# Gated MLP: normalised rows split in row layout and turned by DMA transposes, with three pairs of up banks and two up tiles ahead of the second product

## The reference

```python
x = x + o @ wo
h = shift_token(x)            # second half of the features is taken from the row before
mu = h.mean(-1, keepdims=True)
var = h.var(-1, keepdims=True)
h = (h - mu) / jnp.sqrt(var + 1e-05) * lg + lb
h = h @ w1 + b1               # 256 -> 2 * 682
a, g = jnp.split(h, 2, axis=-1)
h = a * jax.nn.gelu(g, approximate=False)
x = x + h @ w2 + b2           # 682 -> 256
```

## Time and profile before

| what | value |
|---|---|
| median of three executions | 4295.84 us |
| span of the profiled execution | 4300.7 us |
| PE busy in the span | 3849.4 us (90%) |
| DVE, ACT, POOL busy | 3344.8, 2570.4, 1178.2 us |
| first MLP stage | about 1304 to 1508 us of the span |
| second MLP stage | about 1958 to 2161 us of the span |

### The profile page before, as it was taken

The page is one execution under the profiler, slowest core; times in us unless marked ns, Lnnn a source line. Parts: engine busy times, 40 slices in busy tenths (PEclk is TensorE's granted clock), DMA queues, the critical chain, the costliest instruction groups (busy, mean ns, idle before and its releaser), DMA issues. The chain is left out here.

```text
span 4300.7 us, 95101 instructions
## 1 busy us (share of the span) xinstructions
PE 3849.4 (90%) x38420; PEld 2181.8 (51%) x38420; DVE 3344.8 (78%) x5499; ACT 2570.4 (60%) x3473; POOL 1178.2 (27%) x958
## 2 busy tenths in 40 slices
PE   7999999669998969988986899999999999857996
PEld 4788888535555535555553332332333333434764
DVE  5688888769985569985787989999998978585454
ACT  3566666636654335553443777787888888635563
POOL 1122321267761067771140000000000000013552
PEclk9999999889999989999997999999999999978998
DMA  1010100133330033430062000000000000032444
GB/s 63 5 40 28 43 26 25 41 70 65 63 51 28 0 64 65 66 54 8 0 160 47 9 9 1 9 2 2 9 2 2 9 2 9 4 99 76 89 106 104
DMA packets 291062, 167.00 MB, mean 39 GB/s; under 512 B 204692, under 2 KB 281704, under 8 KB 290152
## 3 DMA queue, kind: packets, MB, share of 16 engines
q1 hardware_dynamic: 268040, 125.49, 13.4%
q0 software_dynamic: 13440, 21.24, 2.8%
q10 hardware_dynamic: 9184, 14.68, 1.0%
HBM read 77.81 MB, written 38.58 MB: 27 GB/s over the span
## 5 line engine op out<-in xcount | busy, mean ns | idle before, releaser
L2257 DVE TENSOR_REDUCE s_tops<-ps 128x2 f32<-128x1024 f32 (+3 forms) x1152 | 1251.0, 1131 | 139.9 <-PE ps L2143 101.0
L2226 ACT ACTIVATE s_weights<-ps 128x1024 f32<-128x1024 f32 (+3 forms) x1152 | 1092.6, 952 | 342.2 <-PE ps L2156 191.7
L2178 PE MATMUL ps<-s_weights,v_flat 128*32 128x256 f32 (+1 forms) x8704 | 690.8, 389 | 7.4 <-ACT s_o_t L2232 6.1
L2137 PE MATMUL ps<-keys,s_q 48*128 48x512 f16 (+3 forms) x2304 | 433.3, 373 | 46.9 <-DVE s_tops L2257 27.2
L2156 PE MATMUL ps<-s_q,keys 50*128 50x512 f16 (+3 forms) x2304 | 433.4, 373 | 46.0 <-DVE s_tops L2257 33.6
L2293 POOL CAST s_shift<-s_minus_top 128x16 f16<-128x16 f32 x32 | 6.3, 196 | 1426.8 <-DVE s_minus_top L2264 1426.8
L583 PE MATMUL ps<-a_qt,a_kt 128*128 128x256 f16 x3072 | 375.3, 273 | 3.8 <-POOL s_ones L538 3.8
L2156 PEld LDWEIGHTS ps<-s_q,keys 50*128 50x128 f16 x2304 | 112.2, 93 | 510.1 <-issue 250.1
L1174 PE MATMUL ps<-attention_w,la_yt 128*128 128x512 f16 x1152 | 290.3, 400 | 37.8 <-DMA la_yt<-la_y_parts 30.4
L583 PEld LDWEIGHTS ps<-a_qt,a_kt 128*128 128x128 f16 x3072 | 300.9, 98 | 40.3 <-POOL s_ones L538 4.2
L1249 ACT ACTIVATE la_weights<-ps 128x1024 f32<-128x1024 f32 x124 | 126.8, 1023 | 297.0 <-PE ps L1164 297.0
(11 more groups left out here) (374 smaller groups left out, 7205.5 us busy)
## 6 DMA issues: line engine op xcount, KB each, us to landing
ex_whole<-in_L_ffn_w_dram ACTq DMA_DIRECT2D x14, 1024.0 KB
qk_parts<-a_parts SPq DMA_DIRECT2D x64, 128.0 KB, 4.2
keys<-qk_parts SPq DMA_DIRECT2D x48, 128.0 KB, 5.5
s_q<-qk_parts SPq DMA_DIRECT2D x48, 128.0 KB, 4.7
x<-in_x_dram SPq DMA_DIRECT2D x8, 512.0 KB, 9.4
attention_w<-attention_split SPq DMA_DIRECT2D x2, 2048.0 KB, 9.1
la_table<-in_rotary_dram SPq DMA_DIRECT2D x64, 64.0 KB, 2.1
a_table<-in_rope_dram POOLq DMA_DIRECT2D x8, 512.0 KB, 6.3
```

Of the source, the lines that this page charges most:

```text
L2137: mm = pe.matmul(m.ps[:, bank, 0:width], b.q[rows(half, KEY_PARTS * L1_DH), place % 2, pair, t * P:(t + 1) * P], m.keys[rows(half, KEY_PAR ...
L2178: mm = pe.matmul(m.ps[h * QUAD:(h + 1) * QUAD, OUT, begin:end], m.v_flat[:, first:first + QUAD], weights[:, a % 2, h, begin:end], start=(k ...
L2226: act.activation(weights[:, a % 2, 2 * pair:2 * pair + 2, skip:CHUNK], m.ps[:, bank:end + 1, skip:CHUNK], ACT.Exp).then_inc(s["exp"], 1)
L2257: dve.tensor_reduce(tops[:, u % 2, :, i % 2, t, c], m.ps[:, bank:end + 1, 0:width], AX.X, ALU.max).then_inc(s["max"], 1)
```

## The change

The turn goes from PE to the DMA engines, and three other things move with it.

- `gain` on POOL multiplies `normed` by a row of `ln_g` and adds a row of `ln_b`, in place (two operations of 128x1024 a chunk). For the first chunk DVE does it. Both rows are loaded by SP at the start, replicated on all partitions.
- `high` on ACT casts the chunk to the high f16 part in row layout (`parts`), one operation of 128x1024, behind the gelu of tile 2. `parts_low` on DVE subtracts to get the low part, one operation of 128x1024, behind the gate work of tile 3.
- `turn` on SP waits for `low` and issues 4 DMA transposes, one for each row tile, each of 128 rows by 512 f16 values (128 KB). `up` waits for all four. The shift by one row for the second feature half is now made by reading `ht` one column earlier (`EDGE - k`), and `edge` on POOL copies the column of the row before.
- Banks 0 and 1 are free, so there are three pairs of up banks (`RING = 3`), and PE makes two up tiles of the next chunk ahead of `down` (`AHEAD = 2`).

```diff
-    TURN_AT = ET - 4
+    RING, AHEAD = 3, 2
+    EDGE = 16
+    HIGH_AT, LOW_AT = 2, 3
...
             def _(sp):
+                for to, name in ((lng_row, "ln_g"), (lnb_row, "ln_b")):
+                    sp.dma_start(to[:, :], layer_of(a[name], layer).rearrange("o d -> (o d)").partition_broadcast(P)).then_inc(s["rows_in"], 16)
...
+                def turn(c):
+                    sp.wait_ge(s["low"], c + 1)
+                    if c:
+                        need(sp, s["ht"], 16 * TPC * c)
+                        need(sp, s["a_mm"], ET * (c - 1))
+                    for j in range(TPC):
+                        at = EDGE + j * P
+                        sp.dma_start_transpose(ht[:, c % 2, :, :, at:at + P].rearrange("p a k t -> p (a k) t"),
+                                               parts[:, c % 2, j, :, :].rearrange("p a d -> p (a d)")).then_inc(s["ht"], 16)
+
+                turn(0)
                 move_down(sp, m, s, 1)
                 if not last:
                     load_attention(sp, m, a, layer + 1, s["next_in"])
                 move_up(sp, m, s, 1)
+                for c in range(1, CHUNKS):
+                    turn(c)
...
+                def gain(c, u):
+                    need(pool, s["normed"], c + 1)
+                    whole = normed[:, u, :, :]
+                    pool.tensor_tensor(whole, whole, lng_row[:, :].unsqueeze(1).broadcast_to([P, TPC, D]), ALU.mult).then_inc(s["gained"], 1)
+                    pool.wait_ge(s["gained"], c)
+                    pool.tensor_tensor(whole, whole, lnb_row[:, :].unsqueeze(1).broadcast_to([P, TPC, D]), ALU.add).then_inc(s["whole"], 1)
...
-                def ht_low(c, u):
-                    need(dve, s["a_mm"], ET * (c - 1))
-                    for k in range(KD):
-                        need(dve, s["ht_high"], KD * c + k + 1)
-                        dve.tensor_tensor(ht[:, u, 1, k, :], ht_whole[:, u, k, 0:CHUNK], ht[:, u, 0, k, :], ALU.subtract).then_inc(s["ht"], 1)
+                def parts_low(c, u):
+                    dve.wait_ge(s["high"], c + 1)
+                    dve.tensor_tensor(parts[:, u, :, 1, :], normed[:, u, :, :], parts[:, u, :, 0, :], ALU.subtract).then_inc(s["low"], 1)
...
-                        if e == TURN_AT + 1 and exists(c + 1):
-                            ht_low(c + 1, 1 - u)
+                        if e == LOW_AT and exists(c + 1):
+                            parts_low(c + 1, 1 - u)
...
+                def high(c, u):
+                    if isinstance(c, int) and c == 0:
+                        act.wait_ge(s["first_whole"], 1)
+                    else:
+                        act.wait_ge(s["whole"], c)
+                        need(act, s["ht"], 16 * TPC * (c - 1))
+                    act.copy(parts[:, u, :, 0, :], normed[:, u, :, :]).then_inc(s["high"], 1)
...
-                        if e == TURN_AT and exists(c + 1):
-                            scaled(c + 1, 1 - u)
+                        if e == HIGH_AT and exists(c + 1):
+                            high(c + 1, 1 - u)
...
                 def up(c, u, tiles):
-                    need(pe, s["ht"], KD * (c + 1))
+                    need(pe, s["ht"], 16 * TPC * (c + 1))
...
-                            need(pe, free, ET * c + e - 2 + 1)
+                            need(pe, free, ET * c + e - RING + 1)
...
                 def step(c, u):
-                    up(c, u, range(1, TURN_AT + 1))
+                    up(c, u, range(AHEAD, ET))
                     if exists(c + 1):
-                        turn(c + 1, 1 - u)
-                    up(c, u, range(TURN_AT + 1, ET))
-                    if exists(c + 1):
-                        up(c + 1, 1 - u, range(1))
+                        up(c + 1, 1 - u, range(AHEAD))
                     down(c, u)
```

More of the change, by code:

```diff
@@ L1442, in gated_mlp @@
         after = statistics_buffers(nc, ctx, "gm") if last else None
-        with stage(nc, f"gm{layer}", "weighted", "x", "consts", *(f"x_{n}" for n in STATISTICS), "next_in", "w2_in", "minus", "first", *ROW_STATISTICS, "zeroed", "before", "normed", "turned", "ht_whole", "ht_high", "ht", "a_mm", "g_mm", "gelu",
+        with stage(nc, f"gm{layer}", "weighted", "x", "consts", *(f"x_{n}" for n in STATISTICS), "next_in", "w2_in", "minus", "first", *ROW_STATISTICS, "zeroed", "before", "edge_high", "edge_low", "edge", "normed", "rows_in", "first_gained", "first_whole", "gained", "whole", "high", "low", "ht", "a_mm", "g_mm", "gelu",
                    "hid_whole", "hid_high", "hid", "out", "b2", "y") as (block, s):
@@ L1491, in _ @@
             def _(dve):
-                credit(dve, s["normed"], s["ht"], s["hid_whole"], s["hid"], s["y"])
+                credit(dve, s["normed"], s["hid_whole"], s["hid"], s["y"])
                 def norm(c, u, rows=range(TPC)):
-                    need(dve, s["turned"], KD * (c - 1))
+                    if not isinstance(c, int) or c >= 2:
+                        dve.wait_ge(s["low"], c - 1)
                     for j in rows:
@@ L1615, in _, with hid_high @@
             def _(act):
-                credit(act, s["ht_whole"], s["ht_high"], s["gelu"], s["hid_high"])
+                credit(act, s["gelu"], s["hid_high"])
                 act.wait_ge(s["first"], 1)
-                act.activation(ht_whole[:, 1, 1, CHUNK:CHUNK + 1], m.ps[:, 7, 0:1], ACT.Identity, bias=b.lnb[:, 1:2],
-                               scale=b.lng[:, 1:2]).then_inc(s["before"], 1)
+                act.activation(before[:, :], m.ps[:, 7, 0:1], ACT.Identity, bias=b.lnb[:, 1:2], scale=b.lng[:, 1:2]).then_inc(s["before"], 1)
                 act.wait_ge(s["before"], 1)
[L1623 to L1634, removed]
+                act.copy(ht[:, 0, 0, 1, EDGE - 1:EDGE], before[:, :]).then_inc(s["edge_high"], 1)
+                def high(c, u):
[5 more added lines that the diff above has]
+                    act.copy(parts[:, u, :, 0, :], normed[:, u, :, :]).then_inc(s["high"], 1)
                 def gelus(c, u):
-                    def high(e):
+                    def hid_high(e):
                         need(act, s["hid_whole"], ET * c + e + 1)
@@ L1659, in _ @@
             def _(pe):
[L1660 to L1664, removed]
-                        need(pe, s["ht_whole"], KD * (c - 1) + k + 1)
-                        for j in range(TPC):
-                            t = pe.transpose(m.ps[:, k, j * P:(j + 1) * P], normed[:, u, j, k * P:(k + 1) * P], m.ident[:, :])
-                        t.then_inc(s["turned"], 1)
+                credit(pe, s["a_mm"], s["g_mm"], s["out"])
                 def up_rest(c, u, e):
-                    need(pe, s["gelu"], ET * c + e - 2 + 1)
-                    need(pe, s["hid_whole"], ET * c + e - 2 + 1)
+                    need(pe, s["gelu"], ET * c + e - RING + 1)
+                    need(pe, s["hid_whole"], ET * c + e - RING + 1)
                     terms = [(k, p, q) for k in range(KD) for p, q in TERMS]
@@ L1683, in up @@
                 def up(c, u, tiles):
-                    need(pe, s["ht"], KD * (c + 1))
+                    need(pe, s["ht"], 16 * TPC * (c + 1))
+                    if isinstance(c, int) and c == 0:
+                        pe.wait_ge(s["edge_low"], 1)
+                    else:
+                        need(pe, s["edge"], c)
                     for e in tiles:
```

55 lines of the change are left out of this document (39 added, 16 removed).

## The result

| what | before | after |
|---|---|---|
| median of four executions | 4296.35 us | 4401.71 us (4393.78 to 4403.22) |
| ratio, 95% interval (the quotient of the two medians is 1.0245) | | 1.0234 [1.0221, 1.0246] |
| span of the profiled execution | 4300.7 us | 4401.3 us |
| MLP stage 1, from the `pick` matmul to the end of the last down | 202.9 us | 251.5 us |
| MLP stage 2, the same | 202.3 us | 248.5 us |

Of the 100.6 us between the two spans 94.8 lie in the two MLP stages. Another 4.6 lie behind the second stage, and 1.1 ahead of the first and between the two.

The account below looks back on a forecast made before the run. PE, working nearly without a gap, was taken as the bound. 2 x (17.5 + 31.4 - 2.6) = 92.6 us on the 4300.7 us span, less 4.9 to the median, gave 4388 us; 8 in 10 for 4350 to 4425 us.

Parts of the forecast that it names:

- The wait: Steady chunk, PE before the next chunk's tiles: low part ready at 8.1, transposes landed at 14.4, PE waits 5.2 us.
- the rival of landings that get in each other's way: The four transposes land later, at a slower pitch, adding 2.2 us to each of 14 waits: 4419 us, 12 in 100.
- The clock: Up tiles behind each PE wait run at granted clock 0.50 for about 3.8 us, adding 1.9 us a chunk.
- The rival in which the clock stays: PE waits for the transposes but its clock stays up, 27 us less: 4361 us, 15 in 100.
- Six chunks: Six steady chunks of each MLP stage take 173.4 us in place of 142.0: +31.4 us in each layer.
- The first chunk: Stage start: DVE's first gate 9.9 us later through late `move_down`, then 7.6 more until down is done: +17.5 us a layer.
- The last chunk: End of each stage: no transposes, one full up tile fewer ahead of down, -2.6 us in each layer.
- Odd columns: PE reading `ht` one f16 column early costs 0; rival, such reads take double time: 4503 us, 3 in 100.
- What is hidden: Added POOL operations and changed ACT and DVE work in a chunk are not the bound: no cost either way.
- rule weighed: Skill's 350 to 400 GB/s for transposing DMAs would make PE's wait some 2.4 us; the prediction kept 5.2.

Follow-up runs that it names:

- The run with one transpose: Changed kernel issuing only the last of a chunk's four transposes from chunk 2 on (output incomplete): 4334.63 us, ratio to before 1.0075.
- The filled wait: Changed kernel with 44 matmuls, their result unread, placed where PE waits for the transposes: 4374.14 us, ratio to before 1.0175.
- the kernel in which the gain waits: Kernel with split at tile 0 and reordered start (4309.7 us), plus POOL's gain held until the chunk's `hid` is complete: 4303.04 us.

## Why the prediction was right

The mechanism, the place and the sign were right, and 4401.71 lies in the range given. The median came out 13.7 us above the forecast. By the prediction's steps:

- **The wait.** Low part ready at 8.1: measured 7.9. Wait 5.2: measured 5.4 on the mean of 14. The pitch on SP was 1.27 and not 1.22, the landing 2.5 and not 2.6. The run with one transpose shows that the issue on SP makes some 4 of the 5.4 us. All 64 landings took 2.4 to 3.2 us, so the rival of landings that get in each other's way fell.
- **The clock.** 1.9 us a chunk: the two tiles lost 2.33 in the chunk shown and 1.36 (6.54 - 5.18) in the one at 1347.05, and 1.95 on the mean of all 14. The filled wait gave back 27.6 us against the 27 of the prediction's term. The rival in which the clock stays fell.
- **Six chunks.** +31.4 a layer forecast; measured 176.25 against 141.96, +34.3, in the first stage and 174.04 against 141.96, +32.1, in the second.
- **The first chunk.** +17.5 forecast, +18.6 and +15.9 measured, but the reason given was only partly right. The prediction put 9.9 us on the late `move_down` (its own numbers give 1318.7 - 1308.88 = 9.8). It was 11.0 late, and DVE's first gate, counted from the `pick` matmul, 11.8 and 10.5. Yet making `move_down` first gave back 3.1 us in one stage and nothing in the other. PE's first tile waited 14.90 us for the landing, which was forecast (about 1320, measured 1321.14) and then not taken as a bound of its own. Two causes of nearly the same length stood side by side, so that the sum came out right is in part luck.
- **The last chunk.** -2.6 forecast, -2.6 and -1.5 measured up to the start of down. Not forecast: the last down itself is 1.7 and 0.3 us shorter than before. In the first stage it stands behind a wait of 2.99 us in both kernels, but the granted clock was 0.67 in the 3.1 us behind it before and 1.00 in the 3.4 us behind it after. With this the terms measured add up to the 94.8 of the two stages.
- **Odd columns.** The 24 matmuls at full clock take 5.36 as merged rows in the experiments and 5.34 in the earlier trace rows, half of them reading one column early. No cost beyond these 0.02 us; that rival fell.
- **What is hidden.** In the changed kernel POOL's gain cost nothing in steady chunks: it begins at 1373.11, when DVE's last low part of `hid` has just begun (1373.06, and 0.69 us long as ever). That was timing and not independence. Once the wait for the transposes was taken away the two met.
- **The 13.7 us.** The stages' terms were 2.2 us short (94.8 against 92.6), 5.8 fall outside the stages, where I had forecast nothing, 5.3 come from the step from span to median (I took off 4.9 for a profiled execution that was long, and the one after was 0.4 shorter than its median), and 0.4 are rounding. What makes the 4.6 us behind the second stage stays open; executions of the kernel before alone lie between 4289.89 and 4311.35, so it may be scatter.

Of the rule weighed, the Trainium skill, "Advanced Engine Details and Errata", section X-Bar Transpose (TRN2): 128 KB in each 1.27 us is 103 GB/s here, at the pace of SP's issues, and not 350 to 400, as the local attention's rows had said. The measurement decides.

## What to carry to other kernels

Work taken off the bounding engine pays only if its replacement ends before that engine asks for it: count from the last producer (here a subtraction on DVE) through the issues in a row (four of 1.27 us) and one landing, and start the producer early enough. A wait of 5 us on PE costs more than itself, since the tiles behind it ran at half the clock for some microseconds. Waits of 1.0 to 1.8 us did not do that; of seven between 1.98 and 2.67 us in these runs, three did (1.98 and 2.05 in the long chunk above, and 2.67 in the same chunk of the kernel with one transpose of four). When a large wait is removed, look at once for operations of two engines that it had kept apart, and keep the old form for the one item of a pipeline that has nothing to hide behind, as the first chunk here.

## What the runs showed of the hardware

DVE operations stood still while POOL worked on SBUF tensors beside them. The smallest case is at the start of the stage in the trace after, one column, 0.16 us in the kernel where POOL was idle:

```profile
1313.64 3.19 POOL L1513 TENSOR_TENSOR gm_normed<-gm_normed,gm_lng_row 128x1024 f32<-128x1024 f32 x1 [6.65 <-DVE gm_normed L1543]
...
1314.54 2.31 DVE L1646 TENSOR_TENSOR gm_ht<-gm_before,gm_ht 128x1 f16<-128x1 f32 x1
```

The operations shown as affected read two tensors from SBUF: this one 0.16 to 2.31 us, the low part of `hid` 0.68 to 2.73, the product with the modulation 1.21 to 3.35. The residual, which reads one of its two from PSUM, keeps its 0.42 us in the middle of a POOL operation, as the timeline of the kernel in which the gain waits shows:

```profile
1411.19 2.35 POOL L1503 TENSOR_TENSOR y<-y,b 128x1024 f32<-128x1024 f32 x1
...
1412.60 0.42 DVE L1628 SCALAR_TENSOR_TENSOR y<-ps,y 128x256 f32 x1 [1.44 <-PE ps L1748]
```

The Trainium skill, "SBUF — State Buffer", section SBUF: two separate sides, says that an operation of VectorE with two SBUF inputs and one of GpSimd that reads SBUF take one pair of ports as a lock, each for its whole length. By that rule the traces agree in all four cases. There was one more that its words on two inputs do not cover: a normalisation (L1543), which reads one tensor and a scalar for each row, took 1.55 us in place of 0.33 at 1305.52 beside a MEMSET of POOL that ended at 1306.99. The prediction did not weigh this rule; in the kernel before POOL had one operation of this kind in a chunk.

PE behind a wait of about 5 us ran at 1.2 GHz for 2.4 to 4.1 us of the stretches shown, and matmuls with no use put into the wait kept it at 2.4 GHz.
